# Second expert layer: the shift of the odd slot tiles is made by VectorE, that of the even ones by ScalarE

## The chip, the cores and the metric

The kernel runs on one core of a Trainium2 chip. The metric is the time of one execution on the device in microseconds (us), lower is better; the value quoted is the median of repeated runs. Engines: TensorE (PE, with its weight loads as PEld), VectorE (DVE), ScalarE (ACT), GpSimd (POOL) and SyncE (SP).

## What is computed

Four layers of gated cross attention and feed-forward on 32 x 64 tokens of 256 features. The change lies in the feed-forward part of the second layer, a mixture of eight experts with two chosen per token. Its matrices are rounded to -1, 0, 1, its activations to 8 bits:

```python
def activation_quant(x):
    scale = 127.0 / jnp.maximum(jnp.max(jnp.abs(x), axis=-1, keepdims=True), EPS)
    return jnp.clip(jnp.round(x * scale), -128.0, 127.0) / scale

def bitlinear(x, w):
    ...
    return x_q @ w_q.T

def expert_ffn(x, gw, uw, dw):
    gate = bitlinear(x, gw)
    up = bitlinear(x, uw)
    activated = up * jnp.square(jax.nn.relu(gate))
    return bitlinear(activated, dw)
```

## The kernel before

The program is a row of eight sublayers (attention and feed-forward of four layers), written engine by engine by hand, with semaphores between the engines and nothing that schedules. `layer1_experts` is the sublayer in question. A router picks two of eight experts for each of the 2048 tokens; a sorter gives each (token, expert) pair a place in 39 slot tiles (`NT`) of 128 rows, each tile belonging to one expert. Then the slot loop runs over the tiles j = 0 to 38:

- GpSimd gathers the tile's token rows from memory (`f_got`, L2402), 14 tiles ahead at most, and scatters the tile's result (`f_outputs`, L2410).
- TensorE transposes the rows (`tensor_in`, L2618), multiplies by the gate and the up matrix (`tensor_up`, L2627), transposes the quantized hidden rows (`tensor_turn`, L2635) and multiplies by the down matrix (`tensor_down`, L2643). In round j it does up(j), turn(j-3), down(j-4), in(j+3).
- ScalarE in round j does out(j-5) (`f_y`, L2465), relu(j) (L2446), the shift of tile j-2 (L2452), the copy of the transposed input of tile j+2 (`f_xq`, L2440) and back(j-3) (`f_wholeT`, L2458).
- VectorE for tile j makes `once` = relu x up (L2553), `prod` = once x relu (L2557) and the peak of |prod| along each row (L2561). After an odd tile it makes, for the two tiles of the pair at once, the step, the rate (L2566) and the output scale (three small operations, L2565 to L2567). At every fourth tile, `vector_quad` puts four small operations (L2543 to L2546) between prod and peak.

The shift is `prod * rate + MAGIC`: the product is scaled to 8 bits, and adding the constant MAGIC rounds it. `scalar_back` subtracts MAGIC again after the transposes. The rate of a tile comes with that of its pair, so the shift of an even tile needs the peak of the odd tile behind it. `shifted` has two buffers (j % 2), `prod` has four. All waits are on counting semaphores: `s.rate`, `s.turned`, `s.shifted`. The waits for `s.shifted` are in `tensor_turn` and, for the reuse of `prod`, in `vector_tile`:

```python
act.activation(shifted[:, j % 2, :], prod[:, j % 4, :], ACT.Copy, scale=rate[:, j:j + 1], bias=MAGIC).then_inc(s.shifted, 1)
dve.wait_ge(s.shifted, j - 3)
pe.wait_ge(s.shifted, j + 1)
```

The last layer's feed-forward part uses the same semaphores, counted on from `whole_used`, and makes all its shifts on VectorE (L3429).

Of the kernel before, what the change touches and what calls it, by code (L numbers as in the profile page):

```python
# [7 lines left out]
ACT = mybir.ActivationFunctionType  # L8
ALU = mybir.AluOpType
# [21 lines left out]
MAGIC = 1.5 * 2.0 ** 23  # L31
# [15 lines left out]
def build_program(nc, io):  # L47
    ctx = ExitStack()
    with ctx:
# [2248 lines left out]
        def layer1_experts(before, done):  # L2298
            E, K, I = 8, 2, 512
            IC = I // P  # L2300
            NT = K * TILES + E - 1
# [6 lines left out]
            p, s = Names(), Names()  # L2308
            (
                p.kept0, p.kept1, p.shift, p.rounded, p.rowed, p.mask, p.ranks, p.chain, p.which, p.hot, p.inverse, p.slots,  # L2310
                s.in_ps, s.xq, s.out, s.acc0, s.back0, s.back1, s.back2, s.back3
            ) = early.of("kept0 kept1 shift rounded rowed mask ranks chain which hot inverse slots "
                         "in_ps xq out acc0 back0 back1 back2 back3")
            p.kept = (p.kept0, p.kept1)
            (
                s.raw, s.size, s.total, s.chain, s.gate, s.tern, s.shifted, s.w_tp, s.w, s.up, s.relu, s.once,
                s.prod, s.peak, s.pair, s.rate, s.turned, s.wholeT, s.down, s.acc1
            ) = whole_sems
            s.back, s.acc = (s.back0, s.back1, s.back2, s.back3), (s.acc0, s.acc1)
# [46 lines left out]
            after = whole_used  # L2366
            after.raw, after.size, after.total, after.tern = 0, 6 * E, E, ternary.PER * E
            after.w_tp = after.w = 3 * E
            after.up = after.relu = after.peak = after.wholeT = after.down = after.shifted = after.turned = NT
            after.pair = after.rate = PAIRS  # L2370
            after.acc = TILES
            after.chain = chain0 + 4 * ((NT + QUAD - 1) // QUAD) + PAIRS
            after.tern_signal = s.tern
# [72 lines left out]
                act.activation(relu[:, j % 2, :], bank[1 + j % 2][:, :], ACT.Relu).then_inc(s.relu, 1)  # L2446

            def scalar_shift(act, j):
                act.wait_ge(s.rate, j // 2 + 1)
                if j >= 2:  # L2450
                    act.wait_ge(s.turned, j - 1)
                act.activation(shifted[:, j % 2, :], prod[:, j % 4, :], ACT.Copy, scale=rate[:, j:j + 1], bias=MAGIC).then_inc(s.shifted, 1)  # L2452

            def scalar_back(act, j):
                act.wait_ge(s.turned, j + 1)
# [11 lines left out]
            def scalar(act):  # L2467
                act.wait_ge(*before)
                for i in range(BLOCKS + 2):
                    if i < BLOCKS:  # L2470
                        scalar_norm(act, i)
                    if 1 <= i <= BLOCKS:
                        scalar_turned(act, i - 1)
                    if 3 <= i:
                        router.scalar_keep(act, i - 3)
                    if 2 <= i:
                        router.scalar_logits(act, i - 2)
                router.scalar_keep(act, BLOCKS - 1)
                for q in range(3 * E):
                    scalar_weights(act, q)  # L2480
                    if q == 5:
                        act.wait_ge(router.soft, 2)
                        act.activation(sorter.ex[:, 1:K, :], sorter.ex[:, 1:K, :], ACT.Exp).then_inc(router.exp, 1)
                for j in range(3):
                    scalar_in(act, j)
                for j in range(NT + 5):
                    if 0 <= j - 5:
                        scalar_out(act, j - 5)
                    if j < NT:
                        scalar_relu(act, j)  # L2490
                    if 0 <= j - 2 < NT:
                        scalar_shift(act, j - 2)
                    if 3 <= j + 2 < NT:
                        scalar_in(act, j + 2)
                    if 0 <= j - 3 < NT:
                        scalar_back(act, j - 3)
# [51 lines left out]
            def vector_tile(dve, link, j):  # L2548
# [4 lines left out]
                dve.tensor_tensor(once[:, j % 2, :], relu[:, j % 2, :], bank[3 + j % 2][:, :], ALU.mult).then_inc(s.once, 1)  # L2553
                dve.wait_ge(s.once, j + 1)
                if j >= 4:
                    dve.wait_ge(s.shifted, j - 3)
                dve.tensor_tensor(prod[:, j % 4, :], once[:, j % 2, :], relu[:, j % 2, :], ALU.mult).then_inc(s.prod, 1)  # L2557
                if j % QUAD == 0:
                    vector_quad(dve, link, j)
# [9 lines left out]
            def vector(dve):  # L2569
                dve.wait_ge(*before)  # L2570
                norm.vector_means(dve)
                sorter.vector_tables(dve)
                for i in range(BLOCKS):
                    vector_shift(dve, i)
                    if i == 0:
                        vector_weights(dve)
                for i in range(BLOCKS):
                    vector_rows(dve, i)
                sorter.vector_choose(dve)
                sorter.vector_places(dve)  # L2580
                for k in range(K):
                    sorter.vector_hot(dve, k)
                sorter.vector_which(dve)
                sorter.vector_slots(dve)
                sorter.vector_pay(dve)
                vector_scales(dve)
                link = linker(dve, s.chain, chain0)
                for j in range(NT):
                    vector_tile(dve, link, j)
                assert after.chain == chain0 + link.count[0]  # L2590
                dve.wait_ge(s.out, NT)
                layer2_early.vector(dve)
                vector_combine(dve, K, sorter.share, y_back, s)
                dve.sem_inc(done, TILES)
# [33 lines left out]
                    mm.then_inc(signal, 1)  # L2628

            def tensor_turn(pe, j):  # L2630
                pe.wait_ge(s.shifted, j + 1)
                if j >= 2:
                    pe.wait_ge(s.wholeT, j - 1)
                for c in range(IC):
# [970 lines left out]
```

## Time and profile before

| | |
|---|---|
| median of 3 runs | 1249.22 us (1248.93 to 1250.41) |
| span of the profiled execution, first to last instruction | 1267.6 us |
| busy: PE, DVE, ACT, POOL | 80%, 65%, 48%, 27% |
| slot loop of the second expert layer in the trace | 474.9 to 602 us |
| DVE `f_once` in that loop | 39, mean 685 ns |
| ACT `f_shifted` in that loop | 39, mean 719 ns |

The profiled execution is one execution with the profiler on. Of its own time the profile gives the span; it is 18.4 us above the median of the runs. A share of busy time is an average over all eight sublayers. For this change the slot loop's own rows count.

### The profile page before, as it was taken

What the parts mean: (1) busy time and instruction counts of PE and PEld (TensorE: products, weight loads), DVE (VectorE), ACT (ScalarE), POOL (GpSimd) and SP (SyncE); (2) the same over time, 40 slices, a digit from 0 to 9 for tenths busy, and PEclk for the clock granted to TensorE, in tenths of its full rate; (3) what the DMA queues carried; (4) which work ended last, traced back from release to release, by engine and by line L of the source; (5) the groups of instructions that cost most, each with busy time, mean ns of one, the idle gap of its engine ahead of it and who ended that gap; (6) DMA issues with size and microseconds to landing.
All of it is one profiled execution on the core that took longest, in us unless ns stands there. A gap on an engine that the chain in (4) does not pass through costs nothing.

```text
span 1267.6 us, 20816 instructions
## 1 busy us (share of the span) xinstructions
PE 1011.1 (80%) x6277; PEld 766.7 (60%) x6292; DVE 821.8 (65%) x2015; ACT 603.8 (48%) x1263; POOL 346.7 (27%) x404
## 2 busy tenths in 40 slices
PE   5647989928999767778789999778999999995276
PEld 4436779927777343344446556457888888874154
DVE  6846548845666677777746566567454545588985
ACT  3453257724443576778246665534333323223464
POOL 3197624451000125664231222021111101205200
PEclk8968989968999888989689999979999999995599
DMA  9644457771110001341400000020000010000001
GB/s 288 104 135 131 153 152 225 221 255 37 67 31 1 25 22 49 91 137 58 150 9 18 10 9 8 18 101 26 25 26 24 0 29 25 0 1 1 0 18 50
DMA packets 82274, 86.46 MB, mean 68 GB/s; under 512 B 12236, under 2 KB 75615, under 8 KB 82191
## 3 DMA queue, kind: packets, MB, share of 16 engines
q1 hardware_dynamic: 75662, 68.37, 18.6%
q0 software_dynamic: 6528, 17.04, 4.2%
q8 instruction: 46, 0.75, 0.2%
q14 instruction: 38, 0.30, 0.1%
HBM read 60.52 MB, written 24.85 MB: 67 GB/s over the span
## 4 chain that ended last, share of the span: by engine, by line
PE 55%; DVE 19%; ACT 10%; issue 9%; POOL 3%; DMA 3%; another core or an unknown queue 1%; SPq 1%; DVEq 0%; ACTq 0%; POOLq 0%
PE bank L962 12%; PE bank L983 5%; PE bank L3043 3%; PE bank L1919 2%; PE bank L3084 2%; DVE ln_stat L219 2%; PE bank L2627 2%; PE bank L1945 2%; PE bank L3077 2%; PE bank L2207 1%; PE bank L3028 1%; PE bank L2232 1%; PE bank L3455 1%; DMA f_back<-f_outputs 1%; PE bank L2218 1%
## 5 line engine op out<-in xcount | busy, mean ns | idle before, releaser
L962 PE MATMUL bank<-xhi,whi 128*128 128x512 f32 x256 | 102.0, 398 | 6.0 <-PE bank L983 3.3
L962 PE MATMUL bank<-xlo,whi 128*128 128x512 f32 x256 | 101.0, 395 | 0.0
L962 PE MATMUL bank<-xhi,wlo 128*128 128x512 f32 x256 | 101.0, 394 | 0.0
L877 ACT ACTIVATE ahi<-work 128x512 fp32r<-128x512 f32 x64 | 40.5, 632 | 115.9 <-DVE work L901 115.9
L901 DVE TENSOR_TENSOR work<-work,bank 128x512 f32<-128x512 f32 x64 | 44.0, 688 | 71.6 <-PE bank L962 70.4
L845 POOL TENSOR_TENSOR wlo<-raw,whi 128x1536 fp32r<-128x1536 f32 x8 | 28.1, 3510 | 224.9 <-ACT whi L859 224.9
L983 PE MATMUL bank<-whi,ahi 128*128 128x256 f32 x256 | 73.4, 287 | 13.1 <-DVE alo L903 13.0
L903 DVE TENSOR_TENSOR alo<-work,ahi 128x512 fp32r<-128x512 f32 x64 | 49.2, 768 | 44.7 <-ACT ahi L877 44.7
L874 ACT ACTIVATE work<-bank 128x512 f32<-128x512 f32 x64 | 38.2, 597 | 80.8 <-PE bank L962 80.6
L983 PE MATMUL bank<-wlo,ahi 128*128 128x256 f32 x256 | 72.7, 284 | 0.0
L983 PE MATMUL bank<-whi,alo 128*128 128x256 f32 x256 | 72.7, 284 | 0.0
L2962 DVE TENSOR_REDUCE work<-bank 128x8 f32<-128x512 f32 x64 | 43.7, 683 | 40.1 <-PE bank L3043 39.7
L928 DVE SCALAR_TENSOR_TENSOR resid<-bank,work,resid 128x256 f32<-128x256 f32 x128 | 53.0, 476 | 15.2 <-PE bank L983 15.2
L2818 POOL TENSOR_TENSOR work<-work 128x512 f32<-128x512 f32 x32 | 32.9, 1060 | 102.9 <-ACT work L2845 102.9
L983 PEld LDWEIGHTS bank<-whi,ahi 128*128 128x128 f32 x256 | 48.9, 191 | 19.6 <-issue 17.3
L1624 POOL DMA_INDIRECT f_outputs<-f_y,f_places x39 | 41.3, 1059 | 62.5 <-ACT f_y L1685 39.0
L962 PEld LDWEIGHTS bank<-xhi,whi 128*128 128x128 f32 x256 | 48.1, 188 | 16.6 <-issue 7.3
L2402 POOL DMA_INDIRECT f_got<-f_tokens,f_places x39 | 40.6, 1041 | 55.3 <-DVE f_places L1309 37.8
L962 PEld LDWEIGHTS bank<-xhi,wlo 128*128 128x128 f32 x256 | 48.0, 187 | 11.9
L962 PEld LDWEIGHTS bank<-xlo,whi 128*128 128x128 f32 x256 | 48.2, 188 | 9.2
L219 DVE BATCH_NORM_STATS2 ln_stat<-resid 128x6 f32<-128x256 f32 (+1 forms) x128 | 48.1, 415 | 4.3 <-DVE resid L2980 2.9
L983 PEld LDWEIGHTS bank<-wlo,ahi 128*128 128x128 f32 x256 | 49.0, 191 | 2.0
(513 smaller groups left out, 2995.1 us busy)
## 6 DMA issues: line engine op xcount, KB each, us to landing
f_got<-f_sorted SPq DMA_DIRECT2D x39, 129.0 KB
f_sorted<-clear_row SPq DMA_DIRECT2D x1, 4992.0 KB, 25.5
f_back<-f_outputs SPq DMA_DIRECT2D x18, 256.0 KB, 4.7
raw<-in_L_ffn_w SPq DMA_DIRECT2D x24, 176.0 KB
tern_raw<-in_L_ffn_gate_w SPq DMA_DIRECT2D x8, 512.0 KB
tern_raw<-in_L_ffn_up_w SPq DMA_DIRECT2D x8, 512.0 KB
tern_raw<-in_L_ffn_down_w SPq DMA_DIRECT2D x8, 512.0 KB
ctx_in<-in_ctx SPq DMA_DIRECT2D x32, 128.0 KB
```

The lines of the kernel that those rows point to most:

```text
L219: dve.bn_stats(flat(ln_stat[:, ds(t, 1), :]), x_tile(t)).then_inc(norm_sems[0], 1)
L874: act.activation(silu[0:m, u % 2, :], bank[u % 2][0:m, :], ACT.Silu).then_inc(s.silu, 1)
L877: act.activation(ahi[0:m, u % 2, :], act32[0:m, u % 2, :], ACT.Copy).then_inc(s.ahi, 1)
L901: dve.tensor_tensor(act32[0:m, u % 2, :], silu[0:m, u % 2, :], bank[2 + u % 2][0:m, :], ALU.mult).then_inc(s.hid, 1)
L903: dve.tensor_tensor(alo[0:m, u % 2, :], act32[0:m, u % 2, :], ahi[0:m, u % 2, :].bitcast(F32), ALU.subtract).then_inc(s.alo, 1)
L928: ins = dve.scalar_tensor_tensor(X[:, t, :], bank[4 + 2 * y_slot + k // 2][:, k % 2 * D:k % 2 * D + D], shares_now[:, slot * per + e, t:t ...
L962: mm = pe.matmul(bank[2 * mat + u % 2][0:m, :], up_w(w, slot, mat, c, q), x[:, c, cols], start=j == 0, stop=j == 3 * DC - 1)
L983: mm = pe.matmul(bank[4 + 2 * y_slot + k // 2][:, k % 2 * D:k % 2 * D + D], a[p0:p0 + np_, u % 2, k * P:(k + 1) * P], down_w(w, slot, q, p ...
L1624: pool.indirect_dma_start(g.outputs, bass.IndirectOffsetOnAxis(ap=dest[:, j:j + 1], axis=0), y_out[:, j % OUT_RING, :], None).then_inc(gon ...
L2402: pool.indirect_dma_start(got[:, j, :], None, tokens, bass.IndirectOffsetOnAxis(ap=sorter.token[:, j:j + 1], axis=0)).then_inc(sent[j % FL ...
L2962: dve.tensor_reduce(top[:, x % 2, :], got, AX.X, ALU.max).then_inc(s.top, 1)
L3043: mm = pe.matmul(SOFT[x % 4 + pair][:, :], qT[rows, slot, :], kblk[rows, slot % QB].rearrange("p g k -> p (g k)"), start=True, stop=True)
```

## The change

Odd tiles get their shift from VectorE, right behind the peak of the next (even) tile; ScalarE keeps the even tiles. The semaphore is split into one for even and one for odd tiles, since two engines now raise it, and the count that the last layer starts from is changed with it.

```diff
-                s.in_ps, s.xq, s.out, s.acc0, s.back0, s.back1, s.back2, s.back3
+                s.in_ps, s.xq, s.out, s.acc0, s.back0, s.back1, s.back2, s.back3, s.shifted_odd
...
-                s.raw, s.size, s.total, s.chain, s.gate, s.tern, s.shifted, s.w_tp, s.w, s.up, s.relu, s.once,
+                s.raw, s.size, s.total, s.chain, s.gate, s.tern, s.shifted_even, s.w_tp, s.w, s.up, s.relu, s.once,
...
-            after.up = after.relu = after.peak = after.wholeT = after.down = after.shifted = after.turned = NT
-            after.pair = after.rate = PAIRS
+            after.up = after.relu = after.peak = after.wholeT = after.down = after.turned = NT
+            after.pair = after.rate = after.shifted = PAIRS
...
             def scalar_shift(act, j):
+                assert j % 2 == 0
                 act.wait_ge(s.rate, j // 2 + 1)
                 if j >= 2:
                     act.wait_ge(s.turned, j - 1)
-                act.activation(shifted[:, j % 2, :], prod[:, j % 4, :], ACT.Copy, scale=rate[:, j:j + 1], bias=MAGIC).then_inc(s.shifted, 1)
+                act.activation(shifted[:, 0, :], prod[:, j % 4, :], ACT.Copy, scale=rate[:, j:j + 1], bias=MAGIC).then_inc(s.shifted_even, 1)
+
+            def vector_shift_odd(dve, j):
+                assert j % 2
+                dve.wait_ge(s.rate, j // 2 + 1)
+                if j >= 2:
+                    dve.wait_ge(s.turned, j - 1)
+                dve.tensor_scalar(shifted[:, 1, :], prod[:, j % 4, :], rate[:, j:j + 1], MAGIC, ALU.mult, ALU.add).then_inc(s.shifted_odd, 1)
+
+            def shifted_up_to(eng, j):
+                eng.wait_ge(s.shifted_odd if j % 2 else s.shifted_even, j // 2 + 1)
...
-                    if 0 <= j - 2 < NT:
+                    if 0 <= j - 2 < NT and j % 2 == 0:
                         scalar_shift(act, j - 2)
...
                 if j >= 4:
-                    dve.wait_ge(s.shifted, j - 3)
+                    shifted_up_to(dve, j - 4)
...
                 for j in range(NT):
                     vector_tile(dve, link, j)
+                    if j >= 2 and j % 2 == 0:
+                        vector_shift_odd(dve, j - 1)
...
             def tensor_turn(pe, j):
-                pe.wait_ge(s.shifted, j + 1)
+                shifted_up_to(pe, j)
```

VectorE at the start of the slot loop, before; `f_once` opens a tile, and `f_scratch` is peak, step, rate or scale. The rows begin with tile 2 and end in the small operations behind tile 3:

```order
L2553 TENSOR_TENSOR f_once<-f_relu,bank 128x512
L2557 TENSOR_TENSOR f_prod<-f_once,f_relu 128x512
L2561 TENSOR_REDUCE f_scratch<-f_prod 128x1
L2553 TENSOR_TENSOR f_once<-f_relu,bank 128x512
L2557 TENSOR_TENSOR f_prod<-f_once,f_relu 128x512
L2561 TENSOR_REDUCE f_scratch<-f_prod 128x1
L2565 SCALAR_TENSOR_TENSOR f_scratch<-f_scratch 128x2
L2566 RECIPROCAL f_scratch<-f_scratch 128x2
```

The same place with the change:

```order
L2564 TENSOR_TENSOR f_once<-f_relu,bank 128x512
L2568 TENSOR_TENSOR f_prod<-f_once,f_relu 128x512
L2572 TENSOR_REDUCE f_scratch<-f_prod 128x1
L2460 TENSOR_SCALAR f_shifted<-f_prod,f_scratch 128x512
L2564 TENSOR_TENSOR f_once<-f_relu,bank 128x512
L2568 TENSOR_TENSOR f_prod<-f_once,f_relu 128x512
L2572 TENSOR_REDUCE f_scratch<-f_prod 128x1
L2576 SCALAR_TENSOR_TENSOR f_scratch<-f_scratch 128x2
L2577 RECIPROCAL f_scratch<-f_scratch 128x2
```

The shift of tile 1 now stands between the peak of tile 2 and the first product of tile 3, and the like at every even tile.

ScalarE at the start of the slot loop, rounds 3 and 4, before:

```order
L2446 ACTIVATE f_relu<-bank 128x512
L2452 ACTIVATE f_shifted<-f_prod,f_scratch 128x512
L2440 ACTIVATE f_xq<-bank 128x256
L2458 ACTIVATE f_wholeT<-bank 128x512
L2446 ACTIVATE f_relu<-bank 128x512
L2452 ACTIVATE f_shifted<-f_prod,f_scratch 128x512
L2440 ACTIVATE f_xq<-bank 128x256
L2458 ACTIVATE f_wholeT<-bank 128x512
```

And with the change:

```order
L2446 ACTIVATE f_relu<-bank 128x512
L2440 ACTIVATE f_xq<-bank 128x256
L2469 ACTIVATE f_wholeT<-bank 128x512
L2446 ACTIVATE f_relu<-bank 128x512
L2453 ACTIVATE f_shifted<-f_prod,f_scratch 128x512
L2440 ACTIVATE f_xq<-bank 128x256
L2469 ACTIVATE f_wholeT<-bank 128x512
```

In the odd round the copy of the input follows the relu directly; the even round is as it was. TensorE's order doesn't change.

## Rows read from the trace of the kernel before

**Rows 1.** The page's head: span, and busy time by engine.
```profile
span 1267.6 us, 20816 instructions
...
PE 1011.1 (80%) x6277; PEld 766.7 (60%) x6292; DVE 821.8 (65%) x2015; ACT 603.8 (48%) x1263; POOL 346.7 (27%) x404
```

**Rows 2.** Windows, slot loop: length, busy (x instructions) by engine, PEclk, DMA share, GB/s.
```profile
474.90:602.00 127.10, 95.03 (x527) 53.80 (x536) 93.03 (x217) 93.18 (x194) 72.03 (x71) 0.92 0.29 84
```

**Rows 3.** Groups by line, 474.9 to 602 us: busy us, mean ns, idle before, releasers.
```profile
L2452 ACT ACTIVATE f_shifted<-f_prod,f_scratch 128x512 f32<-128x512 f32 x39 | 28.0, 719 | 4.1 <-issue 1.7 <-DVE f_scratch L2566 1.2 <-PE bank L2635 0.6
L2553 DVE TENSOR_TENSOR f_once<-f_relu,bank 128x512 f32<-128x512 f32 x39 | 26.7, 685 | 27.9 <-ACT f_relu L2446 15.6 <-issue 4.9 <-remote 4.9
```

**Rows 4.** Timeline, tiles 31 to 35: start us, duration us, engine, line, [idle before].
```profile
575.70 0.69 DVE L2553 TENSOR_TENSOR f_once<-f_relu,bank 128x512 f32<-128x512 f32 x1
...
577.15 0.69 DVE L2561 TENSOR_REDUCE f_scratch<-f_prod 128x1 f32<-128x512 f32 x1
...
577.87 0.16 DVE L2565 SCALAR_TENSOR_TENSOR f_scratch<-f_scratch 128x2 f32<-128x2 f32 x1
...
578.21 0.68 DVE L2553 TENSOR_TENSOR f_once<-f_relu,bank 128x512 f32<-128x512 f32 x1
578.27 0.72 ACT L2452 ACTIVATE f_shifted<-f_prod,f_scratch 128x512 f32<-128x512 f32 x1
...
578.90 0.36 ACT L2440 ACTIVATE f_xq<-bank 128x256 bf16<-128x256 bf16 x1
...
579.41 0.27 PE L2618 MATMUL bank<-identb,f_got 128*128 128x128 bf16 x2 [0.23 <-ACT f_xq L2440]
...
580.34 0.69 DVE L2561 TENSOR_REDUCE f_scratch<-f_prod 128x1 f32<-128x512 f32 x1
580.35 0.60 ACT L2446 ACTIVATE f_relu<-bank 128x512 f32<-128x512 f32 x1 [0.24 <-PE bank L2627]
...
580.98 0.69 DVE L2553 TENSOR_TENSOR f_once<-f_relu,bank 128x512 f32<-128x512 f32 x1
...
584.93 0.69 DVE L2561 TENSOR_REDUCE f_scratch<-f_prod 128x1 f32<-128x512 f32 x1
...
586.21 0.69 DVE L2553 TENSOR_TENSOR f_once<-f_relu,bank 128x512 f32<-128x512 f32 x1 [0.59 <-ACT f_relu L2446]
```

**Rows 5.** Timeline, `once` of tiles 21 and 30, with the input copy of 544.63.
```profile
544.63 0.69 DVE L2553 TENSOR_TENSOR f_once<-f_relu,bank 128x512 f32<-128x512 f32 x1 [2.49 <-remote]
544.63 0.38 ACT L2440 ACTIVATE f_xq<-bank 128x256 bf16<-128x256 bf16 x1 [1.02 <-remote]
...
573.50 0.69 DVE L2553 TENSOR_TENSOR f_once<-f_relu,bank 128x512 f32<-128x512 f32 x1 [1.09 <-issue]
```

**Rows 6.** VectorE's scale-and-add in other stages: two groups by form, one timeline row.
```profile
L2521 DVE TENSOR_SCALAR f_rounded<-xn,f_scratch 128x256 f32<-128x256 f32 x8 | 2.3, 349 | 0.1
L3429 DVE TENSOR_SCALAR work<-work 128x1024 f32<-128x1024 f32 x16 | 12.1, 754 | 1.3
...
431.08 1.14 DVE L2521 TENSOR_SCALAR f_rounded<-xn,f_scratch 128x256 f32<-128x256 f32 x4
```

**Rows 7.** Timeline, the drain: peak of tile 38, shift and transposes of tile 37.
```profile
595.38 0.69 DVE L2561 TENSOR_REDUCE f_scratch<-f_prod 128x1 f32<-128x512 f32 x1
595.46 0.72 ACT L2452 ACTIVATE f_shifted<-f_prod,f_scratch 128x512 f32<-128x512 f32 x1
...
596.38 1.08 PE L2635 MATMUL bank<-ident,f_shifted 128*128 128x128 f32 x4
```

**Rows 8.** Timeline, two gathers issued by GpSimd, and VectorE's `prod` at the first.
```profile
531.91 0.69 DVE L2557 TENSOR_TENSOR f_prod<-f_once,f_relu 128x512 f32<-128x512 f32 x1
...
532.24 1.21 POOL L2402 DMA_INDIRECT f_got<-f_tokens,f_places  x1 [0.30 <-issue]
...
535.04 0.97 POOL L2402 DMA_INDIRECT f_got<-f_tokens,f_places  x1 [0.30 <-issue]
```

More of the change, by code:

```diff
@@ L2310, in layer1_experts @@
                 p.kept0, p.kept1, p.shift, p.rounded, p.rowed, p.mask, p.ranks, p.chain, p.which, p.hot, p.inverse, p.slots,
-                s.in_ps, s.xq, s.out, s.acc0, s.back0, s.back1, s.back2, s.back3
+                s.in_ps, s.xq, s.out, s.acc0, s.back0, s.back1, s.back2, s.back3, s.shifted_odd
             ) = early.of("kept0 kept1 shift rounded rowed mask ranks chain which hot inverse slots "
-                         "in_ps xq out acc0 back0 back1 back2 back3")
+                         "in_ps xq out acc0 back0 back1 back2 back3 shifted_odd")
             p.kept = (p.kept0, p.kept1)
             (
-                s.raw, s.size, s.total, s.chain, s.gate, s.tern, s.shifted, s.w_tp, s.w, s.up, s.relu, s.once,
+                s.raw, s.size, s.total, s.chain, s.gate, s.tern, s.shifted_even, s.w_tp, s.w, s.up, s.relu, s.once,
                 s.prod, s.peak, s.pair, s.rate, s.turned, s.wholeT, s.down, s.acc1
```

## The prediction

> **What bounds the kernel now.** First the page's head: all engines together are busy for only part of a span of 1267.6 us, TensorE (PE) for 80% [rows 1]. The change touches the slot loop of the second expert layer alone, so the question is what sets the pace there. The loop runs from the first relu at 474.9 us to about 602 us, that is 127.1 us for 39 tiles, 3.26 us a tile. In that stretch VectorE (DVE) is busy for 93.0 us and ScalarE (ACT) for 93.2 us: neither is full, and they are equally loaded [rows 2]. Next come the groups of instructions. ScalarE's shift, the one that is moved for 19 of 39 tiles, takes 719 ns and its engine hardly waits before it. VectorE's first product of a tile (`once`) has 27.9 us of idle time ahead of it, nearly all of VectorE's idle time in the loop, which looks like ample room [rows 3]. Whether it is room must be read tile by tile.
>
> The timeline of tiles 31 to 35 shows the loop at its best. `once` of tile 31 starts at 575.70, of tile 33 at 580.98 and of tile 35 at 586.21: two tiles in 5.28 and 5.23 us. Followed forward, the chain is a ring: once(31), prod, the peak at 577.15, the pair's scale from 577.87, then ScalarE's shift of tile **30** at 578.27, input copy (`f_xq`) at 578.90, the transposes of the next input at 579.41, its first matmul group, relu(33) at 580.35, once(33) at 580.98 [rows 4]. So the ring goes through the shift of the *even* tile of the pair, in ScalarE's even round. The shift that leaves ScalarE is in the odd rounds, off this ring.
>
> VectorE has a ring of its own that is just as long. From once(31) to once(32) it takes 2.51 us, three long operations and three short ones. From once(32) to once(33), with the four small operations of `vector_quad`, 2.77 us. In the second of these the peak starts at 580.34 and the next `once` 0.64 us later with no idle time marked. In the pair without a quad the peak starts at 584.93 and `once` at 586.21, after 0.59 us of idle time [rows 4]. VectorE is full in every other pair and has about 0.6 us to spare in the others.
>
> **The parts of the change.** *Nineteen shifts leave ScalarE.* Each frees the step from a shift to the input copy behind it, 578.27 to 578.90, so 0.63 us [rows 4]. On the undisturbed ring this is worth nothing: it was in the odd round, where relu(32) came early and waited for VectorE anyway. It can be worth something where VectorE waited at an *even* tile. `once` has marked idle time ahead of it at nine even tiles behind the first (4, 8, 10, 14, 16, 22, 24, 28, 30; at tile 30 it is 1.09 us [rows 5]). Taking the smaller of 0.63 and the wait at each gives 4.7 us as the most; the least is 0. Most of the large waits stand behind late TensorE completions: at tile 21 `once` and the next input copy started together at 544.63, after 2.49 us [rows 5], and an earlier input copy helps nothing there. I take a quarter, **-1.2 us**, nearer to zero because the undisturbed rows show zero.
>
> *Nineteen shifts come to VectorE*, each behind the peak of the next even tile and ahead of the next odd tile's `once`. No row has a 512-element fp32 product and sum with one scalar per partition there. The same operation takes 349 ns for 256 elements and 754 ns for 1024; in a line between them, 0.53 ns an element, 512 elements take 0.48 us. What the engine is held for is less: four of the 256-element ones run in 1.14 us, a step of 0.264 us [rows 6]. Adding 256 x 0.53 ns gives a step of **0.40 us** for 512. The bounds are 0.26 us (the step of the smaller tile) and 0.61 us (the step of its 512-element neighbours, for which the 0.64 us above stands [rows 4]). I take 0.40, as it lies between two rows of the same operation.
>
> *Where that is paid.* At an odd tile the added 0.40 us costs what the idle time ahead of `once` doesn't cover. From tile 3 on, six odd tiles have none marked (5, 9, 29, 31, 33, 37) and tile 25 has 0.24; all others have 0.41 or more. So 6 x 0.40 + 0.16 = **+2.5 us**. What covers the rest are the late completions of TensorE, tile 21 as an example [rows 5]; should they go, the cover goes (first rival).
>
> *The drain.* The last odd shift, of tile 37, ran on ScalarE at 595.46 and ended at 596.18, while VectorE was making the peak of tile 38 from 595.38. The transposes of tile 37 began at 596.38 [rows 7]. Now the shift stands behind that peak and the three small operations of tile 38: by the steps of rows 4 (577.15 to 578.21, 1.06 us) it starts at 596.44 and is done at 596.92, so 0.5 us after the transposes could begin. TensorE is nearly the only engine at work in the tail, so this goes to the end: **+0.5 us**.
>
> *Waits and queues.* The DVE shift waits for a rate that VectorE itself made a tile ago, and for the transposes of two tiles before, which ended about a tile earlier; both are covered. Behind it queue the next `once`, and through it relu's and TensorE's buffers; that is the cost just counted. The split of one semaphore into two adds no instruction on TensorE, since each wait stays one wait. No DMA is added or moved; SyncE's queue is untouched. GpSimd's scatter waits for the output row, which moves with the loop.
>
> **Sum.** +2.5 + 0.5 - 1.2 = +1.8 us. This is a sum against the profiled execution with its span of 1267.6 us. The median of the runs is 1249.22, which is 18.4 us less than that span, so the runs lose less time somewhere, and perhaps in these late completions. The difference is carried over as it is: **1251.0 us**. About 0.2%, 2.5 us, is what a measurement of this kernel can tell from no change; the forecast lies inside.
>
> **The rivals.**
>
> *First, slower: VectorE becomes the bound.* Place: every second pair of tiles, the one with `vector_quad`. There VectorE's own round is 2.51 + 2.77 = 5.28 us and becomes 5.68, longer than ScalarE's and TensorE's ring. In the other pair it stays below: 5.23 less 0.59 plus 0.40. It decides from the point where TensorE's late completions are gone, so that neither of them covers the step. Nine quads follow an odd shift: 9 x 0.40 + 0.5 for the drain = +4.1 us, **1253.3 us**. For it: tiles 29 to 38 run in that way already, and the unprofiled runs are 18.4 us shorter. Against it: idle time of 0.9 to 2.5 us at tiles 13, 17 and 21.
>
> *Second, faster: ScalarE's odd rounds hold the loop.* If all nine even waits end 0.63 us earlier or as far as they go (-4.7), the added step is paid only at 31, 33 and 37 (+1.2), and the drain stays (+0.5): -3.0 us, **1246.2 us**. For it: VectorE waited for relu for most of its 27.9 idle us [rows 3]. Against it: the ring through the even shift, which the change doesn't shorten.
>
> *Third, the shift costs more on VectorE than interpolated.* With the upper bound of 0.61 us the seven places cost 0.21 us more each and the drain 0.2 more: +1.8 + 1.7 = +3.5 us, **1252.7 us**. A way to it: two engines in each other's way. A gather that GpSimd issued at 532.24 took 1.21 us with `prod` running on VectorE from 531.91, another at 535.04, after `prod`, took 0.97 us [rows 8]; an operation with 0.24 us added by such a meeting is about at this bound. Delay of GpSimd itself would cost nothing: gathers run 14 tiles ahead. The Trainium skill (GPSIMD Engine Reference, Specifications) names a contention of GpSimd with VectorE instructions in a two-port mode or with two SBUF inputs. By that rule the new shift would be one more such instruction; rows 8 agree for `prod`, and no row shows it for a shift.
>
> That the change doesn't do what it says is not in question: the order of instructions shows 20 shifts left on ScalarE and 19 on VectorE.
>
> **How the numbers follow.** Forecast, a net between -2.5 and +2.5 us: 0.52. VectorE as the bound: 0.26. A dearer shift: 0.09. ScalarE's rounds: 0.13. Slower is the second and third of these, 0.35; faster 0.13; within 0.2%, 0.52. The range goes from 1247.3, most of the way to the second rival's value and the case that nearly the whole relief is had, to 1254.3, where VectorE is the bound and the shift somewhat over 0.40 us (9 x 0.10 more).
>
> **What would show it.** Right: the DVE shift at about 0.48 us, followed by `once` 0.40 us later than before in the quad pairs of an undisturbed stretch (5.7 us for such a pair, 5.2 for the other); idle time ahead of `once` smaller by about 5 us or more; ScalarE's busy time down by 19 x 0.72 = 13.7 us with more idle time in its place; last `f_y` about 0.5 us later after the last relu. Wrong: an undisturbed quad pair that stays at 5.28 us would mean that VectorE's step was hidden; an undisturbed pair under 5.2 us would mean that the ring doesn't pass through the even shift; a DVE shift of 0.69 us would be the third rival.

## The result and the profile after

| kernel | median | runs | against before |
|---|---|---|---|
| before | 1250.31 us (1247.39 to 1252.21) | 20 | |
| with the change | 1254.40 us (1250.11 to 1259.03) | 20 | 1.0039 (95% interval 1.0026 to 1.0051) |

The change makes the kernel 0.39% slower, 4.1 us by the medians. The forecast had been no change, 1251.0 us, with a range that ended at 1254.3. Of the 3.4 us between forecast and result, 1.1 us is that the kernel before itself came out at 1250.31 and not at 1249.22, from which the forecast had started; the rest is +4.1 us instead of +1.8.

The profile in front of the prediction, with its span of 1267.6 us, doesn't fit runs of 1249 us. It looks like one from a chip on which this kernel takes some 18 us more: a later series on another chip has the kernel before at 1268.72 us, and its traces show the same late waits in the middle of the loop. The record doesn't name the chip of the first profile. So the profile of the changed kernel, with a span of 1250.2 us, can't be set beside the one of 1267.6 us as a whole. For a fair pair the kernel before was profiled once more (first experiment); it has a span of 1245.9 us.

The page's head of the changed kernel, which answers to [rows 1]:

```profile
span 1250.2 us, 20820 instructions
...
PE 1003.2 (80%) x6277; PEld 764.6 (61%) x6292; DVE 829.7 (66%) x2034; ACT 593.8 (48%) x1244; POOL 345.1 (28%) x404
```

VectorE has 19 instructions more and ScalarE 19 fewer. The slot loop as one window, from the first relu to the end of the last `f_y`, answers to [rows 2]:

```profile
470.18:584.41 114.23, 88.34 (x527) 52.53 (x536) 100.14 (x236) 83.29 (x175) 70.50 (x71) 0.95 0.33 93
```

VectorE is busy for 100.1 of 114.2 us. The groups of the same loop (475 to 582 us) show where its idle time has gone, beside [rows 3]:

```profile
L2564 DVE TENSOR_TENSOR f_once<-f_relu,bank 128x512 f32<-128x512 f32 x37 | 25.2, 682 | 2.2 <-ACT f_relu L2446 1.8 <-issue 0.2
L2453 ACT ACTIVATE f_shifted<-f_prod,f_scratch 128x512 f32<-128x512 f32 x20 | 14.4, 721 | 14.3 <-DVE f_scratch L2577 13.7 <-PE bank L2648 0.6
L2460 DVE TENSOR_SCALAR f_shifted<-f_prod,f_scratch 128x512 f32<-128x512 f32 x19 | 9.6, 507 | 0.0
```

Behind its first wait VectorE is idle for 2.2 us ahead of `once` in this window, and ScalarE now waits 13.7 us for VectorE's rate ahead of its shift. The time that ScalarE was given is spent waiting for the engine that was given the work. The timeline of tiles 28 to 31 on VectorE answers to [rows 4]:

```profile
549.46 0.69 DVE L2572 TENSOR_REDUCE f_scratch<-f_prod 128x1 f32<-128x512 f32 x1
550.07 0.48 DVE L2460 TENSOR_SCALAR f_shifted<-f_prod,f_scratch 128x512 f32<-128x512 f32 x1
550.46 0.68 DVE L2564 TENSOR_TENSOR f_once<-f_relu,bank 128x512 f32<-128x512 f32 x1
...
555.00 0.48 DVE L2460 TENSOR_SCALAR f_shifted<-f_prod,f_scratch 128x512 f32<-128x512 f32 x1
555.67 0.69 DVE L2564 TENSOR_TENSOR f_once<-f_relu,bank 128x512 f32<-128x512 f32 x1 [0.20 <-ACT f_relu L2446]
...
561.48 0.67 DVE L2564 TENSOR_TENSOR f_once<-f_relu,bank 128x512 f32<-128x512 f32 x1
```

The shift takes 0.48 us and holds the engine for 0.39 us (550.07 to 550.46): both as interpolated. Its mean is 507 ns, though, because a few of the 19 take longer. The one of 560.92 lies over a scatter that GpSimd issued 0.56 us before:

```profile
560.36 0.97 POOL L2410 DMA_INDIRECT f_outputs<-f_y,f_places  x1 [1.95 <-ACT f_y L2476]
...
560.92 0.63 DVE L2460 TENSOR_SCALAR f_shifted<-f_prod,f_scratch 128x512 f32<-128x512 f32 x1
...
561.48 0.67 DVE L2564 TENSOR_TENSOR f_once<-f_relu,bank 128x512 f32<-128x512 f32 x1
```

Its step is 0.56 us, and that of the shift of 571.91, at the same place behind a scatter, 0.57. But the shift of 484.46, with a gather under way, has a step of 0.40. So the third rival's dearer shift occurs, at two or three of 19 shifts; what brings it about is not shown. The pair from 550.46 to 555.67 has no quad, takes 5.21 us and still has 0.20 us idle. The pair from 555.67 to 561.48 has the quad, takes 5.81 us, with the dearer shift just shown, and has none. Over the loop the nine quad pairs take 5.63 to 6.07 us with a middle value of 5.70, the others 5.18 to 5.31 us with a middle value of 5.21.

### The profile page after: what moved, and what is told of

Its sections match the earlier page's. It is cut to its first block, busy times and chain, and to the rows that moved or that the text cites. A ratio compares the mean times of both kernels' runs of the same rounds, so it can differ in the third digit from the quotient of the medians.

```text
span 1250.2 us, 20820 instructions
## 1 busy us (share of the span) xinstructions
PE 1003.2 (80%) x6277; PEld 764.6 (61%) x6292; DVE 829.7 (66%) x2034; ACT 593.8 (48%) x1244; POOL 345.1 (28%) x404
## 4 chain that ended last, share of the span: by engine, by line
PE 51%; DVE 16%; ACT 8%; issue 7%; POOL 3%; DMA 3%; SPq 0%; ACTq 0%; DVEq 0%; POOLq 0%
PE bank L962 13%; PE bank L983 6%; PE bank L3056 3%; PE bank L1919 3%; PE bank L3097 2%; PE bank L1945 2%; PE bank L3090 2%; DVE ln_stat L219 1%; PE bank L2207 1%; PE bank L3041 1%; DMA f_back<-f_outputs 1%; PE bank L2232 1%; PE bank L3468 1%; PE bank L2640 1%; PE bank L2215 1%
## 6 DMA issues: line engine op xcount, KB each, us to landing
f_got<-f_sorted SPq DMA_DIRECT2D x39, 129.0 KB, 2.4
```

## The experiments

Each run's ratio is to the kernel before on the same chip at the same time. The first four ran together (before: 1249.72 us), the next four on another chip (before: 1268.72 us), the next four (before: 1250.08 us) and the last four (before: 1249.59 us) on a third. "Loop" is from the start of the first relu to the end of the last `f_y`, "drain" from the start of the last relu on, each from one profile.

| run | median us | ratio (95% interval) | loop us | drain us | quad pair, other pair us |
|---|---|---|---|---|---|
| before_again | 1249.95 | 1.0002 (0.9987 to 1.0017) | 109.43 | 9.57 | 5.32, 5.18 |
| relief_only | 1250.64 | 1.0002 (0.9986 to 1.0019) | 108.64 | 9.19 | 5.30, 5.18 |
| load_only | 1252.75 | 1.0021 (1.0007 to 1.0034) | 112.94 | 10.01 | 5.70, 5.21 |
| after_split | 1248.77 | 0.9982 (0.9964 to 1.0000) | 110.52 | 10.26 | 5.28, 5.29 |
| after_again | 1273.67 | 1.0041 (1.0025 to 1.0057) | 129.03 | 10.10 | disturbed |
| after_tail | 1272.36 | 1.0029 (1.0013 to 1.0046) | 129.24 | 9.91 | disturbed |
| before_copyfirst | 1267.63 | 0.9990 (0.9976 to 1.0004) | 127.72 | 9.19 | disturbed |
| before_copyfirst_split | 1267.21 | 0.9988 (0.9968 to 1.0007) | 125.40 | 8.78 | disturbed |
| before_split | 1246.32 | 0.9976 (0.9963 to 0.9990) | 107.92 | 8.64 | 5.23, 5.23 |
| after_split_2 | 1250.15 | 1.0004 (0.9987 to 1.0022) | 109.59 | 9.34 | 5.28, 5.28 |
| before_copyfirst_2 | 1242.19 | 0.9938 (0.9919 to 0.9956) | 103.20 | 9.19 | 5.24, 4.64 |
| before_copyfirst_split_2 | 1244.09 | 0.9949 (0.9933 to 0.9965) | 102.28 | 8.79 | 4.83, 4.83 |
| after_3 | 1253.99 | 1.0038 (1.0021 to 1.0056) | 114.06 | 11.04 | 5.70, 5.22 |
| load_only_2 | 1252.24 | 1.0027 (1.0009 to 1.0045) | 113.32 | 10.13 | 5.69, 5.21 |
| after_tail_2 | 1253.65 | 1.0043 (1.0027 to 1.0059) | 112.59 | 9.97 | 5.70, 5.19 |
| after_copyfirst | 1252.21 | 1.0020 (1.0007 to 1.0033) | 110.39 | 11.33 | 5.63, 4.97 |

The pair times are middle values over the nine pairs of each kind, from one odd tile's `once` to the next.

### The kernel before, profiled again (before_again)

> The kernel before, once more, for an ordinary profile beside the one of 1267.6 us. Both theories: the time is that of before, within 1.5 us. Theory 1 (VectorE's own round bounds the loop with the change): in this trace an undisturbed pair of slot tiles with the four quad operations takes 5.28 us from one odd tile's once to the next, the other pairs 5.2 us, and the loop from the first relu to the last f_y about 109 us, 4 us less than the 113.7 us of the changed kernel. Theory 2 (the added time comes from TensorE's clock or late completions, not from VectorE): the pairs of this trace are as long as those of the changed kernel wherever TensorE is at full clock, and the loop is longer here by less than 1 us or not at all.

The loop as one window:

```profile
470.89:580.32 109.43, 90.66 (x527) 51.40 (x536) 92.25 (x217) 92.36 (x194) 71.27 (x71) 0.96 0.34 97
```

The loop is 4.8 us shorter than the changed kernel's 114.23, as much as the difference in time (4.1 us by the medians, 4.9 by the ratio). Of it, 2.7 us lie ahead of the last relu and 2.1 us in the drain. VectorE at the same tiles, 28 to 31 and on:

```profile
548.19 0.69 DVE L2561 TENSOR_REDUCE f_scratch<-f_prod 128x1 f32<-128x512 f32 x1
548.79 0.68 DVE L2553 TENSOR_TENSOR f_once<-f_relu,bank 128x512 f32<-128x512 f32 x1
...
553.97 0.69 DVE L2553 TENSOR_TENSOR f_once<-f_relu,bank 128x512 f32<-128x512 f32 x1 [0.56 <-ACT f_relu L2446]
...
559.35 0.68 DVE L2553 TENSOR_TENSOR f_once<-f_relu,bank 128x512 f32<-128x512 f32 x1
```

The pair without quad takes 5.18 us and has 0.56 us idle, enough for the 0.39 us step. The pair with quad takes 5.38 us and has none marked (0.1 us of it is a wait too short for a mark, behind the relu of tile 32). That is theory 1's picture. At full clock the pairs differ by kind and not everywhere, which speaks against theory 2: in the stretch from 485 us to the drain both traces show a granted clock of 1.00 (the last number but two of the row):

```profile
485.00:570.00 85.00, 73.63 (x446) 41.84 (x453) 76.10 (x178) 76.54 (x162) 59.69 (x59) 1.00 0.38 111
```

The same stretch of the changed kernel:

```profile
485.00:572.00 87.00, 69.76 (x438) 41.58 (x443) 81.45 (x192) 68.02 (x144) 57.95 (x59) 1.00 0.38 108
```

### The relief alone (relief_only)

```diff
                 for j in range(NT):
                     vector_tile(dve, link, j)
-                    if j >= 2 and j % 2 == 0:
-                        vector_shift_odd(dve, j - 1)
...
             def shifted_up_to(eng, j):
-                eng.wait_ge(s.shifted_odd if j % 2 else s.shifted_even, j // 2 + 1)
+                if j % 2 == 0:
+                    eng.wait_ge(s.shifted_even, j // 2 + 1)
```

(against the changed kernel)

> The shift of the odd tiles is left out altogether, on both engines, and nobody waits for it: ScalarE has the relief, VectorE has no added work. Theory 1: the ring runs through the even shift, so this gains little, 0 to 1 us against before. Theory 2: the odd rounds of ScalarE held the loop at nine even tiles, so this gains 3 to 5 us.

The time doesn't move: 1.0002, and pairs of 5.30 and 5.18 us. The kernel leaves out the odd tiles' shift and the waits for it, so its gain is the most that the relief can bring. Its interval, -1.8 to +2.4 us, excludes theory 2's 3 to 5 us but not a gain of a microsecond; in its trace the loop up to the last relu is 0.4 us shorter than in before_again. Taking 19 shifts from ScalarE is worth nothing measurable. In the trace of the kernel before the change, ScalarE's shift lies in the way of the input copy in every round, but the odd rounds have slack.

### The load alone (load_only, load_only_2)

```diff
                 for j in range(NT):
                     vector_tile(dve, link, j)
+                    if j >= 2 and j % 2 == 0:
+                        dve.tensor_scalar(once[:, j % 2, :], prod[:, (j - 1) % 4, :], rate[:, j - 1:j], MAGIC, ALU.mult, ALU.add)
```

> ScalarE makes all 39 shifts as before; VectorE makes one more product and sum of 512 elements at the place of the odd shift, into a buffer that nobody reads then. Theory 1: the whole price of the change is here, +3.5 to +4.5 us. Theory 2: VectorE has idle time for it, 0 to +1 us.

> VectorE's added operation alone, once more. If the later drain is a part of the price of its own, this stays 1 to 2 us below the changed kernel (+2.5 to +3 us against before); if the difference was chance, both come out within 1 us.

1.0021 and 1.0027; by the medians +3.0 and +2.7 us, where the change has +4.1 and, beside the second of these runs, +4.4. That is below theory 1's +3.5 to +4.5, and clearly above theory 2. The quad pairs go to 5.70 us, the value of the changed kernel, and the others to 5.21. So the added operation alone, with nothing moved, makes the loop at least as slow as the change does up to the last relu: from the relu of tile 5 to that of tile 38 it takes 89.6 and 89.8 us here, 89.4 and 89.1 us in two traces of the changed kernel, and 86.5 us before. The differences, 2.6 to 3.3 us, are about eight quad pairs by 0.38 us (3.0). This is most of the price. The 1.75 us between load_only_2 and the changed kernel beside it lie in the band that had been expected of a drain term; the section on the drain shows why that isn't proof of one.

### Quad work spread (after_split, after_split_2, before_split)

```diff
+            def vector_quad_ahead(dve, link, j):
+                ...
+                link(dve.tensor_tensor(factor[:, four], got_step3[:, four], of_cube[:, four], ALU.mult))
+                link(dve.reciprocal(least[:, four], factor[:, four]))
...
                 if j % QUAD == 0:
                     vector_quad(dve, link, j)
+                if j % QUAD == 2 and j + 2 < NT:
+                    vector_quad_ahead(dve, link, j + 2)
```

`vector_quad` keeps the other two operations; for tile 0 all four are done at once.

> The changed kernel, with two of the four quad operations moved one pair ahead, so that every pair of tiles has two of them: VectorE's round is about 5.3 us in each pair instead of 5.7 and 5.0. Theory 1: at 5.3 against the ring's 5.2 nearly all of the price goes, 0 to +1.5 us against before. Theory 2: VectorE's round plays no part, so the time stays at that of the changed kernel, +3 to +5 us.

> The changed kernel with the split quad once more, beside the one above. Both readings: 0 to 2.5 us under before. It must be clearly under the changed kernel's +4 to +5 us, else VectorE's round was not what cost them.

> The kernel before, with two of the four quad operations moved one pair ahead, and the shifts where they were. The changed kernel with this split was 0.18% under before. Reading a: that gain is the split's own and the moved shift is merely hidden then; here the pairs with quad go from 5.3 to 5.2 us, and the time is 1 to 2.5 us under before. Reading b: the moved shift itself gains something once VectorE's round is even; then this kernel is within 1 us of before and above the split kernel with the moved shift.

With the work even, each pair holds the same VectorE sum. VectorE in after_split, ahead of and at `once` of tiles 29 and 31:

```profile
548.03 0.48 DVE L2460 TENSOR_SCALAR f_shifted<-f_prod,f_scratch 128x512 f32<-128x512 f32 x1
548.42 0.68 DVE L2567 TENSOR_TENSOR f_once<-f_relu,bank 128x512 f32<-128x512 f32 x1
...
553.31 0.48 DVE L2460 TENSOR_SCALAR f_shifted<-f_prod,f_scratch 128x512 f32<-128x512 f32 x1
553.71 0.68 DVE L2567 TENSOR_TENSOR f_once<-f_relu,bank 128x512 f32<-128x512 f32 x1
```

From 548.42 to 553.71 is 5.29 us, against 5.70 and 5.21 by turns. The changed kernel is now as fast as the kernel before: 0.9982 and 1.0004 instead of 1.0039. Nothing about the shift was changed for that, only which pair bears the quad. The split on the kernel before gives 0.9976, so it gains by itself (reading a); reading b falls, since the moved shift is not better than the unmoved one. So the price is not wholly gone: on that chip the split kernel with the moved shift is 3.8 us above the split kernel without it, more than the 5.28 against 5.23 us in the pairs explain (0.05 x 18 = 0.9 us); the drain adds 0.7 us in these two traces, both with a granted clock of 1.00 there. The rest stays open.

### Opening the ring (before_copyfirst, before_copyfirst_split and their second runs)

```diff
-                    if 0 <= j - 2 < NT:
-                        scalar_shift(act, j - 2)
                     if 3 <= j + 2 < NT:
                         scalar_in(act, j + 2)
+                    if 0 <= j - 2 < NT:
+                        scalar_shift(act, j - 2)
```

> The kernel before with one pair of ScalarE's operations exchanged in every round: the copy of the input of tile j+2 ahead of the shift of tile j-2. If the ring runs through the even shift and the input copy behind it, as the prediction has it, the copy no longer waits for the rate and the ring opens: VectorE's own round remains, 5.28 us in the pairs with the four quad operations and about 4.7 in the others, so the loop is 4 to 6 us shorter. If the pace is set by something else, it stays within 1 us of before.

> The exchange of input copy and shift on ScalarE once more. In the earlier run pairs of tiles at the end of the loop took 5.24 and 4.65 us instead of 5.3 and 5.2, but in the middle late TensorE completions took the gain away and the time was only 0.10% under before. Where the middle of the loop is free of them, all 19 pairs should be 5.25 and 4.65, the loop 4 to 5 us shorter, and the time 3 to 5 us under before; where they are there, 0 to 2 us.

> The same exchange, and two of the four quad operations moved one pair ahead. With the ring open and VectorE bounding, spreading the quad work changes VectorE's sum per four tiles little (2 x 4.95 against 5.28 + 4.65), so 0 to 2 us beyond the exchange alone. If instead TensorE or ScalarE bounds the opened loop, no difference.

> Exchange and split together once more, beside the others. Without late completions: pairs of 4.8 us throughout (as at the end of the loop in the earlier run), 2 x 4.8 against 5.25 + 4.65 = 0.3 us per four tiles, so 3 us beyond the exchange alone, 6 to 8 us under before. With them: 0 to 3 us under before.

On the third chip the exchange gives 0.9938, 7.9 us by the medians (six runs), which is more than the 3 to 5 us expected; the loop of the trace is 6.2 us shorter than in before_again. The pairs are the ones expected, 5.24 and 4.64 us, but for one of 6.19 us. VectorE in before_copyfirst_2, `once` of tiles 31, 33 and 35:

```profile
547.12 0.69 DVE L2553 TENSOR_TENSOR f_once<-f_relu,bank 128x512 f32<-128x512 f32 x1
...
552.39 0.68 DVE L2553 TENSOR_TENSOR f_once<-f_relu,bank 128x512 f32<-128x512 f32 x1
...
557.04 0.69 DVE L2553 TENSOR_TENSOR f_once<-f_relu,bank 128x512 f32<-128x512 f32 x1
```

5.27 and 4.65 us, with no idle time marked at any of the three: VectorE is full in both kinds of pair (the pair of 6.19 us has 0.80 us idle, at tile 28). This shows the ring of the prediction: it goes through the even shift and the input copy behind it. Its price was in the other pairs, 5.18 against 4.64 us, and the change could not touch it, since it left the even shift where it was.

On the slower chip the same kernel gained 0.10% (interval 0.9976 to 1.0004). There, late TensorE completions fill the middle of the loop in all four traces, as in the first profile, and the gain shows only from about tile 30 on, where the pairs are 5.24 and 4.65 us too. In two traces of the kernel before, the loop takes 127.1 us in the first profile and 109.4 us in before_again: 17.7 of the 21.7 us by which their spans differ.

The split on top of the exchange makes the pairs even, 4.83 us, but the time is not better: 0.9949 against 0.9938, with intervals that overlap. In sum over four tiles 2 x 4.83 = 9.66 is little below 5.24 + 4.64 = 9.88, 2 us over the loop; the loops of the two traces differ by 0.9 us, and the time shows nothing of it. The exchange alone on the kernel before has the lowest median of all the kernels here, and with the split it is the same within the noise.

### The exchange on the changed kernel (after_copyfirst)

> The changed kernel with ScalarE's input copy ahead of the shift. The ring through ScalarE is then open and VectorE's own round alone is left: with the shift 5.7 us in the pairs with quad and 5.0 in the others, without it 5.25 and 4.65 as the exchange alone showed, so +0.4 in every pair and not only in every second: 19 x 0.4 = 7 us above the exchange alone, which was 7.9 us under before; so -2 to +1 us against before. If VectorE did not bound, it would stay near the exchange alone, 6 to 8 us under before.

Measured +2.6 us against before, above the expected band of -2 to +1. The pairs are as expected, 5.63 and 4.97 us: now both kinds are longer than in the exchange alone, by 0.39 and 0.33 us. Once nothing else bounds, the step is paid in every pair and not only in every second. The groups of its loop, 475 to 582 us:

```profile
L2564 DVE TENSOR_TENSOR f_once<-f_relu,bank 128x512 f32<-128x512 f32 x38 | 25.7, 678 | 0.2 <-issue 0.2
...
L2453 ACT ACTIVATE f_shifted<-f_prod,f_scratch 128x512 f32<-128x512 f32 x20 | 14.4, 721 | 20.2 <-DVE f_scratch L2577 20.2
```

0.2 us of idle time for VectorE, 20.2 us for ScalarE ahead of its shift. The loop is 7.2 us longer than with the exchange alone, 2.1 us of it in the drain (11.33 against 9.19 us, at granted clocks of 0.85 and 1.00). The time differs by 10.0 us between two series; the remaining 3 us are not in this loop and stay open.

### The drain (after_again, after_3, after_tail, after_tail_2)

```diff
-                    if j >= 2 and j % 2 == 0:
+                    if j >= 2 and j % 2 == 0 and j < NT - 1:
                         vector_shift_odd(dve, j - 1)
+                    if j == NT - 2:
+                        vector_shift_odd(dve, j)
```

> The changed kernel once more, on the chip of the three beside it. The changed kernel's own 20 times lie in two heaps, about 1252 and about 1258 us, with a mean granted clock of 0.912 to 0.917 in the first and 0.906 to 0.910 in the second; the kernel with the added VectorE work alone has one heap at 1252.8. Theory 1 (VectorE's round, a later drain, and now and then a longer stretch of TensorE at its lower clock that the later drain brings): the two heaps come again, median +3 to +5 us against before, and an execution with the lower mean clock has its additional half-clock time at the drain of this loop or right behind it. Theory 3 (the second heap has nothing to do with the change): the heaps do not come again, the time is +2.5 to +3 us.

> The changed kernel with one shift at another place: that of tile 37 directly behind its own rate instead of behind the peak of tile 38. Theory 1: the transposes of tile 37 start 0.5 us or more earlier against the last relu, the drain (last relu to the end of the last f_y) goes from 11.7 back towards 10 us, and the time is 0.5 to 2 us under that of the changed kernel. Theory 3: less than 0.5 us.

> The changed kernel beside the next two on the same chip. +4 to +5 us against before if the two earlier comparisons hold.

> The changed kernel with the shift of tile 37 directly behind its rate, once more. With a drain term: 0.5 to 2 us below the changed kernel, close to the added operation alone. Without one: the same as the changed kernel.

The result of the change holds: 1.0041 and 1.0038 on two chips (+5.0 and +4.4 us by the medians). The two heaps of times do not come again: after_3 has twelve times spread from 1249.4 to 1256.9. They were chance or something of that series, and no conclusion here rests on them.

In this pair of profiles the drain is a cost. The drain of the changed kernel, which answers to [rows 7]:

```profile
576.73 0.69 DVE L2572 TENSOR_REDUCE f_scratch<-f_prod 128x1 f32<-128x512 f32 x1
...
577.78 0.48 DVE L2460 TENSOR_SCALAR f_shifted<-f_prod,f_scratch 128x512 f32<-128x512 f32 x1
...
578.32 1.12 PE L2648 MATMUL bank<-ident,f_shifted 128*128 128x128 f32 x4 [0.65 <-DVE f_shifted L2460]
```

The transposes of tile 37 start 1.59 us behind the peak of tile 38. In before_again it is 0.94 us:

```profile
573.72 0.69 DVE L2561 TENSOR_REDUCE f_scratch<-f_prod 128x1 f32<-128x512 f32 x1
...
574.66 0.94 PE L2635 MATMUL bank<-ident,f_shifted 128*128 128x128 f32 x4
```

0.65 us later, where 0.5 had been forecast. The drain as a whole grows by 2.1 us, from 9.57 to 11.68, more than the 0.65 us. TensorE also runs more of it at the lower of its two clock levels: the granted clock of the drain is 0.70 in the changed kernel,

```profile
572.73:584.41 11.68, 7.58 (x38) 4.77 (x36) 5.02 (x13) 6.35 (x13) 4.85 (x5) 0.70 0.16 57
```

and 0.82 in before_again:

```profile
570.75:580.32 9.57, 6.58 (x37) 4.21 (x35) 3.87 (x11) 6.77 (x15) 4.85 (x5) 0.82 0.20 69
```

This clock doesn't belong to the kernel: the same changed kernel has 0.85 in after_3, with a drain of 11.04 us, and 1.00 in after_again, with 10.10 us:

```profile
591.26:601.36 10.10, 5.48 (x38) 3.67 (x36) 5.02 (x13) 6.16 (x13) 4.86 (x5) 1.00 0.18 66
```

Nor does the wait ahead of it explain it: TensorE waits 1.80 or 1.81 us for the even shift of tile 36 in all three. What makes the clock fall in one execution and not in another was not tried. With the tail edit the drain is 9.97 us and the loop 1.5 us shorter than in after_3, but at a clock of 1.00 against 0.85. At the same clock of 1.00, after_tail has 9.91 us and after_again 10.10: the place of that one shift is worth 0.2 us there. Against the kernel before (9.57 and 9.55 us, both at 0.82) the drain of the changed kernel is longer in every trace, by 0.5 us (after_again, at 1.00) to 1.5 (after_3, at 0.85) and 2.1 us. The times agree with a small term: 1.0029 against 1.0041 in one series, 1.0043 against 1.0038 in the other. So a drain term is seen in the traces, its size goes with a clock that differs from execution to execution, and only 0.2 us of it has been traced to the place of the last shift; the intervals, +-2 us wide, would hardly show a term of 1 us.

## Why the prediction was wrong

**What held.** The ring through the even shift (opened by the exchange: 5.18 to 4.64 us). VectorE's own round as the other bound, 5.28 us in the pairs with quad. The interpolated cost, 0.48 us and a step of 0.40: measured 0.48 and 0.39 for most of the shifts. The place of the cost where nothing disturbs, in every second pair: 5.32 to 5.70 us, others 5.18 to 5.21. The later transposes in the drain, 0.65 us for 0.5.

The first rival named the mechanism and said 9 x 0.40 + 0.5 = +4.1 us; the medians differ by 4.1 us. That the two agree so well is partly luck: in the trace the loop differs by 4.8 us, with 2.7 where it had 3.6 and 2.1 where it had 0.5. Three of the signs came out of another size than forecast: the idle time ahead of `once` fell by 3.6 us from before_again to the changed kernel (10.9 to 7.3) and not by 5; ScalarE's busy time in the loop by 9.1 us (92.36 to 83.29) and not by 13.7, although the row of the shift itself fell by 13.6 (28.0 to 14.4); the last `f_y` came 2.1 us later after the last relu and not 0.5.

**What failed.** The terms of the sum, set beside the traces from the chips on which the kernel takes 1250 us (each run against before_again, one trace each):

| term | forecast us | ahead of the last relu, traces us |
|---|---|---|
| added shifts on VectorE | +2.5 | +3.1, +3.3 (load_only, load_only_2) |
| relief of ScalarE | -1.2 | -0.4 (relief_only) |
| both | +1.3 | +2.7, +3.2 (after, after_3) |

The step that failed is the count of places where the added step is paid: late completions were to cover it at all but seven odd tiles. The term beside it, a relief that pays for half of the cost, was mis-sized. The drain, forecast at +0.5, is +2.1 and +1.5 us in the traces of after and after_3, at differing clocks.

*The relief of -1.2 us.* "I take a quarter" of the 4.7 us that the waits at nine even tiles allowed. relief_only shows none in the time, 1.0002 with an interval from -1.8 to +2.4 us, and 0.4 us in the trace; and the changed kernel, which has the relief, is not faster than load_only, which has none. So -1.2 was too much, though the time alone doesn't exclude it. The text had said itself that the undisturbed ring was worth nothing here, and then gave a part of the disturbed waits to the change.

*The cover of the late completions.* The added step was counted at six odd tiles and not at nine quads and more, because idle time stood ahead of `once` at the others in a trace of 1267.6 us. In the traces of the chips with 1250 us these waits are absent: 5.8 us of idle time ahead of `once` behind the first tile in before_again, where that trace had 22.8. The span being 18.4 us above the median of the runs was read as something to be "carried over as it is", though the late completions in this loop were just about the place where it could lie. It should have made the undisturbed stretch, tiles 30 to 38, the one to scale up, as the first rival did. With 0 for the relief and nine quads the sum is +4.1, the rival's.

Where the late completions are, the trace and the time disagree. In the trace of after_again, beside the first profile, which has such waits too, they do cover: the loop goes from 127.1 to 129.0 us, +1.9, and the idle time ahead of `once` from 27.9 to 22.3 us, 5.6 less, which takes in most of 19 x 0.39 = 7.4 us.

```profile
L2564 DVE TENSOR_TENSOR f_once<-f_relu,bank 128x512 f32<-128x512 f32 x39 | 26.7, 684 | 22.3 <-ACT f_relu L2446 16.5 <-issue 5.8
```

That is the forecast's own +1.8. But the time on that chip is 1.0041, +5.0 us by the medians, and the profiled execution is the fastest of the twelve, which spread from 1269.1 to 1280.4 us. Single traces of executions that differ so much can't decide it; where the 5 us go on that chip stays open.

The chances had 0.35 on slower, and 0.26 on the mechanism that it was. The range ended 0.1 us short, and its end was itself 0.1 us above its own sum (1249.22 + 4.1 + 0.9 = 1254.2).

## What to carry to other kernels

When an engine shows idle time, ask for each wait whether its releaser is part of a ring that goes through this engine or a disturbance that another chip or run may not have; before a trace's waits are used as cover, see whether its span agrees with the times to be predicted; here it didn't, by 18.4 us. Moving work from one engine to another helps only if the moved step lies on the ring that sets the pace: here the even shift did, the odd one didn't, and exchanging two instructions of one engine (copy first, 0.62% faster on one chip and 0.10% on the disturbed one) or spreading four small ones (0.24% faster) did what the moved shifts could not. An added step is paid in the rounds in which its engine is already full, and is free in the others; so count an engine's work round by round and not on average. Before a difference between two traces is given to a change, see whether the same kernel shows it between two of its own executions: here the drain did, with clocks from 0.70 to 1.00.

## What the runs showed that had not been expected

- The same kernel takes 1250 us on two chips and 1268.7 us on another. In the traces 17.7 us lie in this one loop (127.1 against 109.4 us), in waits of about 1 to 3 us that end behind TensorE's work in the middle of it. In the first profile, for example, the matmuls of `tensor_up` for tile 21 are recorded until 541.86 and `once` starts at 544.63. They last until about tile 30, which is where GpSimd's last gathers are issued. What causes them was not tried.
- One added VectorE operation of 0.48 us in every second tile costs about 3 us in all (3.0 and 2.7 by the medians), and leaving out 19 ScalarE operations of 0.72 us gains nothing that the times show (-1.8 to +2.4 us).
- When the input copy no longer waits behind the shift, VectorE runs with hardly any marked idle time from tile to tile. In before_copyfirst_2, behind the first pair, the pairs repeat within 0.01 and 0.07 us (4.64 and 4.65; 5.23 to 5.30), but for the one of 6.19.
- The granted clock of the drain differs between executions of the same changed kernel (0.70, 0.85 and 1.00), and with it the length of the drain (11.68, 11.04 and 10.10 us).
